# Turning the first two tiles on TensorE and computing the modulation as columns, in an adaLN block with a mixture-of-experts feed-forward

## The chip, the cores and the metric

The kernel runs on one core of one Trainium2 chip. The metric is the device time of one execution in microseconds (us). The engines are TensorE (PE; its weight loads are shown apart as PEld), VectorE (DVE), ScalarE (ACT), GpSimd (POOL) and SyncE (SP), which here only issues DMAs. Each engine works through its own instruction list in order; the lists meet in semaphores alone.

## The reference, cut to what matters

There are 4 batches of 1024 tokens with 512 channels, all in f32. A vector per batch gives six modulation vectors, two normalised inputs are shifted and scaled by them, and two branches are gated by them.

```
mod = silu(c) @ wmod                       # (4,512) @ (512,3072): sa, ca, ga, sb, cb, gb
ga, gb = clamped to |g| >= 0.25
h = layernorm(x) * (1 + ca) + sa
q, k, v = relu(h Wq), relu(h Wk), h Wv     # 16 heads of 32
vk = [v, 1]^T k over the tokens of a batch;  out = (vk q) / (its last row)
x = x + ga * (out Wproj + b)
h = layernorm(x) * (1 + cb) + sb
x = x + gb * (top-2-of-8 experts(h) + shared expert(h))
```

## The kernel before

Tokens are cut into 32 tiles of 128 (TILES; BT = 8 tiles make a batch). Numbers that enter a projection are split into a high and a low f16 part, so one product is three f16 matmuls (split_matmul, L85 to L89). The low part is what DVE (or POOL) subtracts after ACT wrote the high part.

All five engines run a written-out loop over slots s. In slot s PE projects tile s (project_k, project_v, project_q), then adds its keys and values into vk (sum_keys_values). From slot 9 on it also attends for tile t = s - 9 and projects out for tile t - 1. From slot 32 on the shared expert runs beside the last attention tiles, then alone, and the last stage runs 71 tiles of 128 expert slots: e_up, e_turn (three f32 transposes on PE), e_down.

The way of tile i to PE: DVE takes its statistics (stats) and writes (x - mean) * (1 + ca) (centre), ACT multiplies by the deviation (scale), POOL adds sa (shift), ACT writes the high part (h_high), DVE the low part (h_low), SP issues a transposing DMA into ht (turn_h). rows_f holds ca and sa of a batch, spread over all partitions. In slot s the engines do this for tile s + 2. DVE's list in a slot is q_low(s-1), centre(s+2), stats(s+3), k_low(s), h_low(s+2), v_low(s), and sum_keys_values(s) on PE waits for k_low(s) and v_low(s):

```
            pe.wait_ge(m.k_lo, i + 1)
            pe.wait_ge(m.v_lo, i + 1)
```

The start: four DMAs bring the first 1024 columns of wmod. PE multiplies them by silu(c) of batch 0 repeated over 128 columns (L1279), which gives sa and ca already spread over the partitions, in f32 matmuls that each show as two passes. It then computes modulation rows 0 and 1 for all four batches (modulate, L1238: weights 128x4, 512 columns stream through). Rows 2 and 3 follow in slot 3 and rows 4 and 5 in slot 4, each row in 4 matmuls, after sum_keys_values; ACT and DVE copy and clamp them as tiles of 4x512. In slot 6 SP stores them to DRAM and loads them back spread over the partitions (load_rows_b), then loads the first out-projection weights, and only then issues the transposing DMA of tile 8:

```
        if s == 6:
            sp.wait_ge(m.mod_step, 12)
            ...
            load_rows_b(0)
            load_xr(0)
            for k in (0, 1):
                load_wp(0, k)
        turn_h(s + 2)
```

The twelve pieces of the query, key and value weights (128x512 each) arrive in a ring and are split by ACT (split_high, L977) and DVE (split_low, L591) between the other work of the first slots. vk_low(b) on DVE (L525) writes the low part of a batch's vk at the end of slot 8(b+1), and attend in the next slot waits for it.

## Time and profile before

| what | us |
|---|---|
| median of 3 runs | 1217.57 |
| lowest and highest run | 1216.61 and 1219.41 |
| the profiled execution, its own time | 1217.89 |
| its span in the trace | 1216.1 |
| PE busy in the span | 1189.8 |
| DVE, ACT, POOL busy | 805.9, 417.7, 506.3 |

The span is what the trace covers; the execution's own time is 1.79 us longer. Busy time adds up stages with different limits, so it says which engine is the fullest and nothing about a single stage. Matmuls are pipelined, so a matmul's recorded duration is longer than the distance to the next one; the distance is what counts in a sum.

### The profile page before, as it was taken

The numbers are of one execution on the slowest core, as the hardware profiler recorded it, in microseconds if no ns is written. First come the engines' busy times: TensorE is split into PE (matmuls) and PEld (weight loads), VectorE is DVE, ScalarE is ACT, GpSimd is POOL, SyncE is SP. The second block draws the span as 40 slices with busy tenths as digits, with TensorE's granted clock in tenths as the row PEclk, the third lists the DMA queues.
The fourth block names the chain that finished last, engine by engine and source line by source line (L and its number), as shares of the span: only waits on it lengthen the run. The fifth ranks groups of instructions, "written<-read, shape, count | busy, mean of one in ns | idle before, by whom it ended". The sixth has DMA issues, their size and how long they took to land.

```text
span 1216.1 us, 25326 instructions
## 1 busy us (share of the span) xinstructions
PE 1189.8 (98%) x9054; PEld 776.8 (64%) x9054; DVE 805.9 (66%) x1578; ACT 417.7 (34%) x873; POOL 506.3 (42%) x409
## 2 busy tenths in 40 slices
PE   7999999999999999999999999999999999999996
PEld 2646666666666666767777777656666666666663
DVE  5647778878776777655857754266666666666665
ACT  4424444445443432333323323222222222222221
POOL 2212566656564554222112112345445554455543
PEclk9999999999999999999999999999999999999998
DMA  7816597998788978745434535579787897779783
GB/s 238 228 40 168 125 250 192 214 234 212 182 222 185 229 209 197 173 99 120 122 87 104 137 85 117 111 150 135 132 141 140 131 132 139 138 135 136 133 127 45
DMA packets 253255, 185.27 MB, mean 152 GB/s; under 512 B 186496, under 2 KB 198784, under 8 KB 253132
## 3 DMA queue, kind: packets, MB, share of 16 engines
q1 hardware_dynamic: 217368, 114.40, 42.1%
q0 software_dynamic: 20512, 45.62, 22.4%
q10 hardware_dynamic: 15256, 23.62, 6.7%
q8 instruction: 79, 1.29, 0.4%
q14 instruction: 40, 0.33, 0.1%
HBM read 87.07 MB, written 52.75 MB: 115 GB/s over the span
## 4 chain that ended last, share of the span: by engine, by line
PE 90%; DVE 2%; issue 2%; DMA 2%; POOL 1%; ACT 1%; SPq 0%; ACTq 0%; POOLq 0%; DVEq 0%
PE ps_o L87 7%; PE ps_o L89 7%; PE ps_o L88 7%; PE ps_vs L87 6%; PE ps_vs L88 6%; PE ps_vs L89 6%; PE ps_kh L87 4%; PE ps_vh L87 4%; PE ps_vh L88 4%; PE ps_vh L89 4%; PE ps_kh L88 4%; PE ps_kh L89 4%; PE ps_qh L87 4%; PE ps_qh L89 4%; PE ps_qh L88 4%
## 5 line engine op out<-in xcount | busy, mean ns | idle before, releaser
L444 POOL DMA_INDIRECT out<-y,slot_row x71 | 139.3, 1963 | 190.3 <-DVE y L882 138.7
L89 PE MATMUL ps_o<-w_all,xt 128*128 x568 | 177.5, 313 | 0.0
L88 PE MATMUL ps_o<-w_all,xt 128*128 x568 | 177.5, 313 | 0.0
L87 PE MATMUL ps_o<-w_all,xt 128*128 x568 | 177.5, 312 | 0.0
L874 DVE SCALAR_TENSOR_TENSOR gate_row<-gate_rows,batch_weight,gate_row 128x512 f32<-128x512 f32 x213 | 158.9, 746 | 2.5
L368 POOL DMA_INDIRECT out<-s_sum,row_no x32 | 53.8, 1680 | 197.6 <-DVE s_sum L623 192.0
L1133 ACT ACTIVATE at<-ps_y 128x384 f16<-128x384 f32 x71 | 34.8, 491 | 250.7 <-PE ps_y L1353 247.1
L330 POOL TENSOR_TENSOR h<-cen,rows_f 128x512 f32<-128x512 f32 x32 | 40.6, 1270 | 130.6 <-ACT cen L901 115.4
L89 PE MATMUL ps_qh<-ht,wqkv 128*128 128x128 f16 x512 | 87.4, 219 | 0.0
L88 PE MATMUL ps_qh<-ht,wqkv 128*128 128x128 f16 x512 | 87.4, 219 | 0.0
L87 PE MATMUL ps_qh<-ht,wqkv 128*128 128x128 f16 x512 | 87.4, 219 | 0.0
L864 DVE SCALAR_TENSOR_TENSOR a<-ps_o,a 128x352 f32<-128x352 f32 x71 | 37.3, 525 | 73.9 <-PE ps_o L89 72.6
L431 POOL DMA_INDIRECT g<-h_d,slot_token x71 | 71.9, 1013 | 31.9 <-issue 21.0
L882 DVE TENSOR_TENSOR y<-ps_vs,gate_row 128x512 f32<-128x512 f32 x71 | 49.1, 692 | 52.6 <-PE ps_vs L89 51.7
L87 PE MATMUL ps_vs<-w_all,at 128*128 (+1 forms) x213 | 80.9, 380 | 2.9 <-DVE at L869 2.9
L598 DVE SCALAR_TENSOR_TENSOR s_act<-ps_vh,s_act 128x256 f32<-128x256 f32 x32 | 13.6, 424 | 102.7 <-ACT s_act L984 102.6
L89 PE MATMUL ps_vs<-w_all,at 128*128 (+1 forms) x213 | 80.6, 378 | 0.0
L88 PE MATMUL ps_vs<-w_all,at 128*128 (+1 forms) x213 | 80.6, 378 | 0.0
L89 PEld LDWEIGHTS ps_o<-w_all,xt 128*128 128x128 f16 x568 | 55.6, 98 | 29.1
L88 PEld LDWEIGHTS ps_o<-w_all,xt 128*128 128x128 f16 x568 | 55.5, 98 | 26.4
L87 PEld LDWEIGHTS ps_o<-w_all,xt 128*128 128x128 f16 x568 | 55.4, 98 | 25.5
L87 PE MATMUL ps_kh<-s_ht,sh 128*128 128x256 f16 x256 | 69.8, 272 | 0.1
(251 smaller groups left out, 3341.2 us busy)
## 6 DMA issues: line engine op xcount, KB each, us to landing
w_stage<-in_w_d ACTq DMA_DIRECT2D x64, 176.0 KB
xb<-in_x SPq DMA_DIRECT2D x32, 256.0 KB, 3.7
xr<-in_x SPq DMA_DIRECT2D x32, 256.0 KB, 4.0
out<-x SPq DMA_DIRECT2D x32, 256.0 KB, 3.6
h_d<-hl SPq DMA_DIRECT2D x32, 256.0 KB, 2.5
h2t_d<-h2t SPq DMA_DIRECT2D x32, 256.0 KB, 3.5
s_ht<-h2t_d SPq DMA_DIRECT2D x32, 256.0 KB, 3.6
sstage<-in_sh_flat SPq DMA_DIRECT2D x32, 136.0 KB, 3.6
```

What stands on the lines that cost most here:

```text
L87: nc.tensor.matmul(out, lh, rh, start=first, stop=False, skip_group_check=True)
L88: nc.tensor.matmul(out, lh, rl, start=False, stop=False, skip_group_check=True)
L89: return nc.tensor.matmul(out, ll, rh, start=False, stop=last, skip_group_check=True)
L330: pool.tensor_tensor(m.h[:, i % 2, :], m.cen[:, i % 2, :], m.rows_f[:, (i // BT) % 2, SA, :], ALU.add).then_inc(m.h_done, 1)
L368: pool.indirect_dma_start(m.out, bass.IndirectOffsetOnAxis(ap=m.row_no[:, t:t + 1], axis=0), m.s_sum[:, u, :], None, compute_op=ALU.add).t ...
L431: pool.indirect_dma_start(m.g[r][:, :], None, m.h2_d, bass.IndirectOffsetOnAxis(ap=m.slot_token[:, t:t + 1], axis=0)).then_inc(m.gathered[ ...
L444: pool.indirect_dma_start(m.out, bass.IndirectOffsetOnAxis(ap=m.slot_row[:, t:t + 1], axis=0), m.y[:, t % Y_RING, :], None, compute_op=ALU ...
L598: v.scalar_tensor_tensor(out=m.s_act[:, q % 2, :], in0=m.ps_h[j % 3][:, 1, :], scalar=1.0 / SCALE, in1=m.s_act[:, q % 2, :], op0=ALU.mult, ...
L864: v.scalar_tensor_tensor(out=m.a[:, t % 2, 0:INTER], in0=m.ps_h3[:, 0:INTER], scalar=1.0 / SCALE, in1=m.a[:, t % 2, 0:INTER], op0=ALU.mult ...
L874: v.scalar_tensor_tensor(out=row, in0=m.gate_rows[:, b, :], scalar=m.batch_weight[:, b, t:t + 1], in1=row, op0=ALU.mult, op1=ALU.add).then ...
L882: v.tensor_tensor(m.y[:, t % Y_RING, :], m.ps_ey[:, 0:C], m.gate_row[t % GW_RING][:, :], ALU.mult).then_inc(m.ey_ready, 1)
L1133: act.activation(m.at[:, t % 2, 0, :, :], m.ps_a[:, :, :], ACT.Copy).then_inc(m.e_at_hi, 1)
```

## The change

Tiles 0 and 1 no longer go through POOL's shift and the transposing DMA. DVE normalises them (normalise), PE turns the result with four f32 transposes (turn_n), and DVE applies scale and shift as per-partition numbers, since a channel is now a partition (modulate_turned). ACT and DVE (POOL for tile 1) write the two f16 parts straight into ht.

For that the modulation is computed turned. A chunk of wmod (128x128, f32) is now the weight, and the four columns of silu(c) stream through. There are 96 such matmuls: 32 at the start, which give sa and ca, and 64 that are issued one by one behind each split_matmul of the projections of tiles 3, 4 and 5 (modulate_beside). Clamps and products work on 128x16. The rows that later stages need are made by one PE transpose each, in slot 0 and, for the rest, in slot 6 after project_v (turn_modulation), copied by ACT and then stored by SP. rows_f of batch 0 is made by POOL (a diagonal matrix) and PE (spread_rows) and copied by DVE and ACT.

The order of the first slots is written out anew. PE runs turn_n(1) and spread_rows(SA) after project_v(0). SP loads all twelve weight pieces through a ring of 8. DVE handles splits 0 to 11, k_low(0) and stats(2) ahead of the slot loop, with modulate_turned(1) between splits 8 and 9.

Three waits move at other places: vk_low of the last batch stands earlier in slot 32; the buffer at is two buffers, of which only the second waits for the shared expert's end; and the last e_turn is issued inside the e_down before it. The diff, cut to its core:

```diff
-X_RING, QT_RING, HT_RING, XR_RING, X2_RING, H2T_RING, STAGE_RING, W_RING = 4, 10, 3, 2, 3, 3, 6, 4
+X_RING, QT_RING, HT_RING, XR_RING, X2_RING, H2T_RING, STAGE_RING, W_RING = 4, 10, 3, 2, 3, 3, 8, 4
...
-CONSTS = 5
-SPLITS_FIRST = {-2: (4,), -1: (6,), 0: (10, 11)}
-SPLITS_LAST = {-2: (5,), -1: (7, 8, 9)}
+IDENT_READY, MODT_READY, V_READY, HEADS_READY = 3, 5, 7, 12
+PE_TURNED = 2
+MOD_GROUP, MOD_GROUPS, MODT = 8, 3, 32
+MOD_FROM, MOD_STEPS = 3, 24
...
+    for n in range(KC, 2 * KC):
+        sp.dma_start(m.stage[:, n, :], m.pieces[n][0]).then_inc(m.stage_loaded[n], 16)
     load_x(2)
+    for n in range(2 * KC, 3 * KC):
+        sp.wait_ge(m.stage_lo, n - STAGE_RING + 1)
+        sp.dma_start(m.stage[:, n % STAGE_RING, :], m.pieces[n][0]).then_inc(m.stage_loaded[n % STAGE_RING], 16)
...
         if s == 6:
-            sp.wait_ge(m.mod_step, 12)
-            sp.dma_start(m.mod_d[:, 2 * C:6 * C], m.mod[:, 2 * C:6 * C]).then_inc(m.mod_stored, 16)
-            sp.dma_start(m.gab_d, m.gate_tmp[:, 0:C]).then_inc(m.mod_stored, 16)
-            sp.wait_ge(m.mod_stored, 48)
+            sp.wait_ge(m.modrow_copied, 2)
+            sp.dma_start(m.mod_f_d.rearrange("b (c n) -> (b c) n", n=P), m.modrow[:, 1, :]).then_inc(m.mod_stored, 16)
+            sp.wait_ge(m.mod_stored, 32)
...
+        if s == -2:
+            pool.wait_ge(m.mod_copied, 2)
+            for r, cols in ((CA, SCALE_A), (SA, SHIFT_A)):
+                pool.tensor_tensor(m.diag[:, r, :, :], m.ident[:, :].unsqueeze(1).to_broadcast([P, KC, P]),
+                                   m.modt[:, 0, cols].unsqueeze(2).to_broadcast([P, KC, P]), ALU.mult).then_inc(m.diag_done, 1)
+        if s == -1:
+            pool.wait_ge(m.h_hi, 2)
+            pool.tensor_tensor(m.ht[:, 1, KC:2 * KC, :], m.h[:, 1, :].rearrange("p (k n) -> p k n", k=KC), m.ht[:, 1, 0:KC, :],
+                               ALU.subtract).then_inc(m.h_lo, 1)
...
+    def normalise(i):
+        v.wait_ge(m.rstd_done, i + 1)
+        v.tensor_scalar(m.cen[:, i, :], m.xb[:, i, :], m.mv[:, i, 0:1], m.rstd[:, i, :], ALU.subtract, ALU.mult).then_inc(m.cen_done, 1)
+
+    def modulate_turned(i):
+        v.wait_ge(m.n_turned, i + 1)
+        for k in range(KC):
+            op = v.tensor_scalar(m.h[:, i, k * P:(k + 1) * P], m.ps_n[i][:, k, :], m.modt[:, 0, 4 + k:5 + k], m.modt[:, 0, k:k + 1], ALU.mult, ALU.add)
+            op.then_inc((m.scaled, m.h_half, m.h_half, m.h_done)[k], 1)
+
+    def turned_low(half):
+        part = slice(2 * half, 2 * half + 2)
+        v.wait_ge((m.h_half_hi, m.h_hi)[half], 1)
+        v.tensor_tensor(m.ht[:, 0, KC + 2 * half:KC + 2 * half + 2, :], m.h[:, 0, :].rearrange("p (k n) -> p k n", k=KC)[:, part, :],
+                        m.ht[:, 0, part, :], ALU.subtract).then_inc((m.h_half, m.h_lo)[half], 1)
...
+    stats(0)
+    normalise(0)
+    split_low(0)
+    split_low(1)
+    v.wait_ge(m.mod_done, 1)
+    v.wait_ge(m.consts, MODT_READY)
+    v.tensor_scalar(m.modt[:, :, SCALE_A], m.ps_mod[0][:, SCALE_A, :].rearrange("p c b -> p b c"), 1.0, None, ALU.add).then_inc(m.mod_copied, 1)
+    v.tensor_copy(m.modt[:, :, SHIFT_A], m.ps_mod[0][:, SHIFT_A, :].rearrange("p c b -> p b c")).then_inc(m.mod_copied, 1)
+    v.wait_ge(m.mod_copied, 2)
+    modulate_turned(0)
+    split_low(2)
+    turned_low(0)
+    split_low(3)
+    turned_low(1)
+    split_low(4)
+    split_low(5)
+    stats(1)
+    split_low(6)
+    split_low(7)
+    normalise(1)
+    split_low(8)
+    modulate_turned(1)
+    for n in range(9, 12):
+        split_low(n)
+    k_low(0)
+    stats(2)
+    for s in range(TILES + TAIL):
         t = s - LAG
-        if s == -3:
-            v.wait_ge(m.silu_done, 1)
-            for k in range(KC):
-                v.tensor_copy(m.sct_rep[:, k, :], m.sct[:, k, 0:1].to_broadcast([P, P])).then_inc(m.rep_done, 1)
-        if s == -2:
-            v.wait_ge(m.bc_done, 2)
-            v.tensor_scalar(m.rows_f[:, 0, CA, :], m.ps_o[:, 1, :], 1.0, None, ALU.add).then_inc(m.row0_done, 1)
+        if s == 0:
+            v.wait_ge(m.bc_done, 1)
+            v.tensor_copy(m.rows_f[:, 0, CA, :], m.ps_row[CA]).then_inc(m.row0_done, 1)
...
+        if s == TILES:
+            vk_low(B - 1)
         h2_low(t - 2)
-        for n in SPLITS_LAST.get(s, ()):
-            split_low(n)
         v_low(s)
...
-        if 0 < s <= TILES and s % BT == 0:
+        if 0 < s < TILES and s % BT == 0:
...
+    def turned_high(i, part, ready, done):
+        act.wait_ge(ready, i + 1)
+        act.activation(m.ht[:, i, part, :], m.h[:, i, :].rearrange("p (k n) -> p k n", k=KC)[:, part, :], ACT.Copy).then_inc(done, 1)
...
+    turned_high(0, slice(0, 2), m.h_half, m.h_half_hi)
+    turned_high(0, slice(2, 4), m.h_done, m.h_hi)
+    for n in range(KC, 2 * KC + 1):
+        split_high(n)
...
+    k_high(0)
+    turned_high(1, slice(0, 4), m.h_done, m.h_hi)
+    for n in range(2 * KC + 1, 3 * KC):
+        split_high(n)
...
+        if s in m.mod_slots:
+            g = m.mod_slots[s]
+            chunks = slice(MOD_GROUP * g, MOD_GROUP * (g + 1))
+            act.wait_ge(m.mod_done, g + 1)
+            act.activation(m.modt[:, :, chunks], m.ps_mod[g][:, :, :].rearrange("p c b -> p b c"), ACT.Copy).then_inc(m.mod_copied, 1)
+        if s in m.turn_slots:
+            r = m.turn_slots[s]
+            act.wait_ge(m.modrow_done, r + 1)
+            act.activation(m.modrow[:, r, :], m.ps_modrow[r], ACT.Copy).then_inc(m.modrow_copied, 1)
...
-        if t == 0:
+        if t == 1:
...
+            if i < PE_TURNED:
+                pe.wait_ge(m.h_lo, i + 1)
+            else:
+                pe.wait_ge(m.ht_loaded[i % HT_RING], ht_use(i))
             at_least(pe, m.k_lo, i)
-            if i == 0:
-                pe.wait_ge(m.stage_lo, KC)
             for k in range(KC):
+                if i == 0:
+                    pe.wait_ge(m.stage_lo, k + 1)
                 mm = split_matmul(nc, m.ps_k[:, :], (m.ht[:, i % HT_RING, k, :], m.ht[:, i % HT_RING, KC + k, :]),
                                   (m.wqkv[:, k, 0, C:2 * C], m.wqkv[:, k, 1, C:2 * C]), k == 0, k == KC - 1)
-            mm.then_inc(m.k_done, 1)
+                if k == KC - 1:
+                    mm.then_inc(m.k_done, 1)
+                modulate_beside(i, k)
...
+    def modulate(n):
+        g, k, c = n // (MOD_GROUP * KC), n // MOD_GROUP % KC, n // (MOD_GROUP * KC) * MOD_GROUP + n % MOD_GROUP
+        if g == 0 and n % MOD_GROUP == 0:
+            pe.wait_ge(m.wmod_loaded[k], 16)
+        if g > 0 and n % (MOD_GROUP * KC) == 0:
+            pe.wait_ge(m.wmod_loaded[KC + g - 1], 16 * KC)
+            pe.wait_ge(m.h_done, PE_TURNED)
+            pe.wait_ge(m.modrow_copied, 1)
+        mm = nc.tensor.matmul(m.ps_mod[g][:, n % MOD_GROUP, :], m.wmod[:, k, c * P:(c + 1) * P], m.sct[:, k, :],
+                              start=k == 0 and c == MOD_GROUP * g, stop=k == KC - 1, skip_group_check=True)
+        if (n + 1) % (MOD_GROUP * KC) == 0:
+            mm.then_inc(m.mod_done, 1)
+
+    def modulate_beside(i, step):
+        n = MOD_GROUP * KC + MOD_STEPS * (i - MOD_FROM) + step
+        if MOD_FROM <= i and n < MOD_GROUPS * MOD_GROUP * KC:
+            modulate(n)
+
+    def turn_n(i):
+        pe.wait_ge(m.consts, IDENT_READY)
+        pe.wait_ge(m.cen_done, i + 1)
         for k in range(KC):
-            pe.wait_ge(m.wmod_loaded[KC * (j // 2) + k], 16)
-            mm = nc.tensor.matmul(m.ps_mod[j], m.sct[:, k, :], m.wmod[:, k, j * C:(j + 1) * C], start=k == 0, stop=k == KC - 1)
-        mm.then_inc(m.mod_done, 1)
+            mm = nc.tensor.transpose(m.ps_n[i][:, k, :], m.cen[:, i, k * P:(k + 1) * P], m.ident[:, :])
+        mm.then_inc(m.n_turned, 1)
+
+    def spread_rows(r):
+        pe.wait_ge(m.diag_done, 1 if r == CA else 2)
+        nc.tensor.matmul(m.ps_row[r], m.one[:, :], m.diag[:, r, :, :].rearrange("p k n -> p (k n)"), start=True, stop=True).then_inc(m.bc_done, 1)
+
+    def turn_modulation(r):
+        mm = nc.tensor.transpose(m.ps_modrow[r], m.modt[:, :, :].rearrange("p b c -> p (b c)"), m.ident[:, :])
+        mm.then_inc(m.modrow_done, 1)
...
-    pe.wait_ge(m.rep_done, KC)
-    for k in range(KC):
-        pe.wait_ge(m.wmod_loaded[k], 16)
-        for r in (0, 1):
-            mm = nc.tensor.matmul(m.ps_o[:, r, :], m.sct_rep[:, k, :], m.wmod[:, k, r * C:(r + 1) * C], start=k == 0, stop=k == KC - 1)
-            if k == KC - 1:
-                mm.then_inc(m.bc_done, 1)
-    modulate(0)
-    pe.wait_ge(m.row0_done, 2)
-    modulate(1)
+    pe.wait_ge(m.silu_done, 1)
+    for n in range(MOD_GROUP * KC):
+        modulate(n)
+    turn_n(0)
+    spread_rows(CA)
 
     for s in range(TILES + TAIL):
         t = s - LAG
         project_k(s)
         project_v(s)
+        if s == 0:
+            turn_n(1)
+            spread_rows(SA)
+        if s == 6:
+            pe.wait_ge(m.mod_step, 12)
+            turn_modulation(1)
...
-        for j in m.mod_slots.get(s, ()):
-            if j == 2:
-                pe.wait_ge(m.row0_done, 2)
-            if j == 3:
-                pe.wait_ge(m.mod_copied, 2)
-            if j >= 4:
-                pe.wait_ge(m.mod_copied, j - 1)
-            modulate(j)
+        if s == 0:
+            pe.wait_ge(m.h_done, PE_TURNED)
+            turn_modulation(0)
...
+    def e_down(t, expert, turn_within=False):
         pe.wait_ge(m.e_at_lo, t + 1)
         at_least(pe, m.ey_ready, t)
         for k in range(IT):
+            if turn_within and k == 1:
+                e_turn(t + 1)
...
-    pe.wait_ge(m.consts, CONSTS)
     expert = expert_of(0)
     e_up(0, expert)
     down(CHUNKS - 1)
...
         e_up(t, following)
         if t == 1:
             pe.wait_ge(m.s_t1_done, 2 * CHUNKS)
-        e_down(t - 1, expert)
+        e_down(t - 1, expert, t == SLOT_TILES - 1)
         expert = following
-    e_turn(SLOT_TILES - 1)
...
+    m.at = [(sb, region(GATE_AT, ACT_AT))[j](f"at{j}", [P, 2, IT, P], F16) for j in range(2)]
...
+        m.mod_slots, m.turn_slots = {4: 1, 5: 2}, {0: 0, 6: 1}
```

## Rows read from the trace of the kernel before

**Rows 1.** Chain that ended last, first 26 us: start us, length us, what.

```profile
5.89 10.12 PE ps_o L1279 x16
...
16.77 0.76 DVE cen L486
...
18.36 1.27 POOL h L330
19.66 0.64 ACT hl L908
...
21.04 4.33 DMA ht<-hl
25.41 0.46 PE ps_kh L87
```

**Rows 2.** Busy: PE, PEld, DVE, ACT, POOL; then granted clock, DMA share, GB/s.

```profile
25.40:28.90 3.50, 3.48 (x9) 1.29 (x10) 3.50 (x6) 1.72 (x4) 0.38 (x2) 0.53 0.99 238
```

**Rows 3.** The same chain, slots of tiles 0 to 6.

```profile
32.46 0.06 PE ps_qh L87
...
35.14 0.06 PE ps_vs L1197
...
35.82 0.22 PE ps_kh L87
...
44.37 0.22 PE ps_kh L87
...
77.08 6.96 PE ps_o L1238 x16
...
92.69 0.22 PE ps_kh L87
```

**Rows 4.** PE weight loads in time: start us, length us, line, tiles, form.

```profile
11.15 0.33 PEld L1279 LDWEIGHTS ps_o<-wmod,sct_rep 128*128 128x128 f32 x1 [0.52 <-issue]
11.98 0.19 PEld L1279 LDWEIGHTS ps_o<-wmod,sct_rep 128*128 128x128 f32 x1 [0.50 <-issue]
```

**Rows 5.** PE weight loads by shape: count, busy us, mean ns, idle before.

```profile
L89 PEld LDWEIGHTS ps_qh<-ht,wqkv 128*128 128x128 f16 x512 | 50.1, 98 | 0.0
...
L1238 PEld LDWEIGHTS ps_o<-wmod,sct 128*4 128x4 f32 x32 | 2.6, 87 | 9.8 <-issue 9.6
```

**Rows 6.** PE matmuls in order of time, router logits of one tile.

```profile
307.26 0.17 PE L1231 MATMUL ps_o<-gate,h2t 128*128 128x16 f16 x1
...
307.44 0.17 PE L1232 MATMUL ps_o<-gate,h2t 128*128 128x8 f16 x1
```

**Rows 7.** DVE groups by line and shape.

```profile
L497 DVE SCALAR_TENSOR_TENSOR k_sb<-ps_kh,k_sb 128x512 f16<-128x512 f32 x32 | 22.1, 690 | 12.2 <-ACT k_sb L914 12.1
...
L537 DVE TENSOR_SCALAR den<-ps_o 128x16 f32<-128x16 f32 x32 | 5.3, 164 | 0.0
```

**Rows 8.** DVE in order of time, a split while POOL works.

```profile
23.58 1.34 DVE L591 SCALAR_TENSOR_TENSOR wqkv<-stage,wqkv 128x512 f16<-128x512 f32 x1 [0.30 <-ACT wqkv L977]
```

**Rows 9.** SP's DMA issues in slot 6: start us, length us, line, tiles.

```profile
94.47 0.29 SPq L265 DMA_DIRECT2D gab_d<-gate_tmp  x1
96.96 0.34 SPq L202 DMA_DIRECT2D rows_ga<-mod_d  x1
...
100.24 1.24 SPq L161 DMA_TRANSPOSE ht<-hl  x1
```

**Rows 10.** Tile ht, the transposing DMA issued at 100.24 us alone.

```profile
DMA to landing us min/median/max: 6.5/6.5/6.5
```

**Rows 11.** Tile ht, all its DMAs of the first 140 us.

```profile
DMA to landing us min/median/max: 3.0/4.1/8.7
```

**Rows 12.** PE waits, 354 to 450 us: waiter, releaser, total, times, longest.

```profile
PE ps_o L87 <- DVE vk L525: 2.5, 1, 2.5
```

**Rows 13.** Waits of the whole span, one of ScalarE.

```profile
ACT gate_row L1139 <- DMA gate_rows<-mod_d: 12.2, 1, 12.2
```

**Rows 14.** The same chain, last 20 us, its last turn.

```profile
1203.28 0.34 PE ps_y L1353 x3
```

More of the change, by code:

```diff
@@ L64 @@
 VK_OPS = 6
-MODS = 6
 class Parts:
@@ L89, in split_matmul, with ht_use @@
     return nc.tensor.matmul(out, ll, rh, start=False, stop=last, skip_group_check=True)
+def ht_use(i):
+    return 16 * len(range(i % HT_RING if i % HT_RING >= PE_TURNED else i % HT_RING + HT_RING, i + 1, HT_RING))
 def rows_of(dram, i):
@@ L157, in turn_h @@
     def turn_h(i):
-        if tile(i):
+        if tile(i) and i >= PE_TURNED:
             sp.wait_ge(m.h_lo, i + 1)
@@ L326, in shift @@
     def shift(i):
-        if tile(i):
+        if tile(i) and i >= PE_TURNED:
             pool.wait_ge(m.scaled, i + 1)
@@ L371, in gpsimd_program @@
     step(pool.memset(m.minus_half[:, :], -0.5))
+    step(pool.memset(m.ident[:, :], 0.0))
+    step(pool.affine_select(out=m.ident[:, :], in_=m.ident[:, :], compare_op=ALU.not_equal, fill=1.0,
+                            base=0, pattern=[[-1, P]], channel_multiplier=1))
+    step(pool.memset(m.one[:, :], 1.0))
+    step(pool.memset(m.modt[:, :, :], 0.0))
     step(pool.memset(m.v_sb[:, :, 0, :, P:P + 1], SCALE))
@@ L480, in centre @@
     def centre(i):
-        if tile(i):
+        if tile(i) and i >= PE_TURNED:
             if i % BT == 0 and i:
@@ L663, in vector_program @@
         stats(s + 3)
-        if s == -3:
-            for n in range(KC):
-                split_low(n)
-        for n in SPLITS_FIRST.get(s, ()):
-            split_low(n)
         if s == 1:
@@ L897, in scale @@
     def scale(i):
-        if tile(i):
+        if tile(i) and i >= PE_TURNED:
             act.wait_ge(m.cen_done, i + 1)
```

165 lines of the change are left out of this document (68 added, 97 removed).

## The prediction

> **What bounds the kernel now.** I read the page first: TensorE is busy for nearly the whole span, so a part of the change counts for what it does to TensorE's list, and other engines count where TensorE waits for them. The chain of waits then shows three places that the change touches. At the start it runs through the first f32 matmuls on TensorE, VectorE, ScalarE, GpSimd, ScalarE, VectorE and a transposing DMA, and the first projection begins at 25.41 us [rows 1]. From there it stays on TensorE, 8.55 us a tile (35.82 to 44.37), broken only by the wide modulation matmuls of slots 3 and 4, 6.96 us each [rows 3]. The waits name one stall further on, 2.5 us for vk_low of the last batch [rows 12]. The end hangs on the last e_turn and what follows it [rows 14].
>
> The sum is made against the profiled execution, 1217.89 us, whose span is 1216.1 us. The median of the three runs is 1217.57 us, so what the sum changes is put on that. Within 0.2% (2.4 us) this kernel's measurement can hardly tell a change from none.
>
> **A thin f32 pass.** The new modulation loads 128x128 f32 weights and streams four columns. No row shows that shape. A weight load of 128 f32 columns took 0.19 us, one of 4 columns 0.087 us [rows 4, 5], so the part that grows with columns is 0.103 us, 0.107 us for 128. The early load of 0.33 us [rows 4] is longer by about twice that part; while TensorE runs at the lower of its levels I take 0.213 us. The rest of a load overlaps its neighbours: f16 loads last 0.098 us [rows 5], yet eight f16 passes of 16 and 8 columns with such loads start within 0.18 us, 0.026 us apart [rows 6]. That 0.026 is the lower bound for the distance of two thin passes, the full 0.19 (0.33) the upper; I take 0.107 (0.213), since the durations follow the columns.
>
> **The first group.** Removed: 16 passes of 512 columns that gave sa and ca, and 16 for modulation rows 0 and 1. Added: 32 matmuls, 64 thin passes, which can start at the same 5.89 us [rows 1]. The load row changes from 0.33 to 0.19 us by 11.98 us [rows 4]; if the level rises there again, 29 passes are done by then and 35 follow at 0.107: the group ends at 15.8 us. Bounds: 64 at 0.026 and its double give 7.6 to 9.2 us, 0.33 then 0.19 gives 20.6 us.
>
> **From there to the first projection.** Four transposes and their latency, 0.75 us (three take 0.34 [rows 14]). Four VectorE operations on 128x128, between 0.164 and 0.69 us each [rows 7]; I take 0.28, started 0.2 apart: 0.9. Then split_low(2), half of the low part, split_low(3), the other half: about 1.95 us by the 0.69 of 128x512. GpSimd makes the two diagonals meanwhile, and a split took 1.34 us beside GpSimd's work [rows 8]; I add 0.6 (0 to 1.3). Project_k(0) starts 4.2 us after the group, at 20.0 instead of 25.41. GpSimd's diagonal (1.27 [rows 1]) and spread_rows(CA) fit into these 4.2 us.
>
> **What is late next.** Project_k(0) and project_v(0) took 25.41 to 32.46, 7.05 us [rows 1, 3], so they now end at 27.0, 5.4 us earlier. Only then does turn_n(1) stand in TensorE's list, and VectorE, in order, is stopped at modulate_turned(1) until it is done. Behind that instruction are queued splits 9 to 11, k_low(0), stats(2), the copy of rows_f, centre(2), stats(3), h_low(2) and, last, v_low(0), for which sum_keys_values(0) waits. Counted from the end of project_v(0): transposes 0.64; four operations, 1.5; ScalarE's high part of tile 1 and split 9 at 0.64 each [rows 1], 2.8; three splits on VectorE, 4.65; k_low, 5.25; stats, 6.25; copy, 6.95; centre(2) to the end of h_low(2) took 16.77 to 21.04, 4.27 us [rows 1], 11.2; v_low, 11.8; with GpSimd beside it 12.2. TensorE has project_q(0) in between (waiting for splits 10 to 12) and then nothing for some 5 us. Before, this distance was 32.46 to 35.14, 2.7 us [rows 3]. So sum_keys_values(0) starts at 39.2 instead of 35.14: 4.05 us later. After the wait ahead of the first projection TensorE's granted clock was 0.53 for 3.5 us [rows 2]; the new wait is longer, so I count that loss once more, 3.5 x 0.47 = 1.65. The start costs 5.7 us. Its bounds follow from the group's end, and from 0 to 1.65 for the clock.
>
> The weight loads by SP cost nothing: project_v and project_q still wait for VectorE's splits. Tile 2's transposing DMA is issued 11.2 us after project_v(0) and needed some 22 us after it, so even 8.7 us to landing [rows 11] is covered.
>
> **Modulation beside the projections.** Removed: two groups of 16 wide passes, 13.92 us [rows 3]. Added: 64 matmuls. 24 stand behind matmuls of 512 columns, which hide the first load; exposed are 0.107 and two floors of 0.026, 0.16 us each. 40 stand behind matmuls of 128 columns, 0.055 apart, which hide half the first load: 0.107 + 0.052 + 0.052, 0.21 us each. 3.8 + 8.4 = 12.2 us, a gain of 1.7 us. At 0.026 a pass it is 3.3 us (gain 10.6), at 0.19, with 0.05 for the floors, it is 24 x 0.24 and 40 x 0.38 less what 0.055 hides, 20.8 (loss 6.9). The shorter clamps are work of VectorE while TensorE is the bound: nothing.
>
> By the Trainium skill, "TensorE: Matmul & The Clock Gate", section "LDWEIGHTS (loading the stationary operand)", a load takes its columns divided by 1.2 in ns, an estimate of 107 ns for 128 columns, with no word of the engine's level. The rows agree at the higher level and show about twice as much at the lower one [rows 4]. By the rule the sum below would come to +0.5 instead of +3.5 us, because the first group would end at 12.7 us. The section "Weight-path perf modes — Fast Weight Load (FWL) and DoubleRow" says that the fast load is not used for f32 weights; that speaks against the first rival.
>
> **Slot 6.** SP's store waited only for VectorE's clamps and went out 1.8 us after project_k(6) began (94.47 against 92.69 [rows 3, 9]). Now turn_modulation(1) comes after project_v(6), 5.2 us, and ScalarE copies it behind v_high and sh_high: 6.6 us. From store to tile 8's transposing DMA SP took 94.47 to 100.24, 5.8 us [rows 9], so that is issued at 12.4 and, with the 6.5 us to landing of this very DMA [rows 10], lands at 18.9. Project_k(8) is due after two tiles, 17.1. Loss 1.8 us; 0 at the median landing of 4.1, 3.7 at 8.7 [rows 11] and a bit of latency. Rows_b and the out-projection weights come later too, but are not needed for two more slots.
>
> **The moved waits.** Vk_low early in slot 32 ends the stall of 2.5 us [rows 12]: VectorE has the value from ScalarE by then, and nothing else is late at that attend. Gain 2.5, at worst 0. The two at buffers: nothing, because ScalarE is held there by the load of the gate rows anyway, its one wait of 12.2 us [rows 13]. The last e_turn, 0.34 us [rows 14], is earlier on TensorE, but VectorE reads its result only after e_out of the tile before, which now waits for 0.34 us more of TensorE: loss 0.2 (0 to 0.4).
>
> **Sum.** 5.7 - 1.7 + 1.8 - 2.5 + 0.2 = +3.5 us: 1221.4 for the profiled execution, 1221.1 for the median.
>
> **Rivals.**
> First, faster: the thin passes flow as the f16 ones do. At 0.026 the group ends 6.6 us earlier and slots 3 to 5 save 8.9 more, 1205.6 us. For it: loads are taken ahead and f16 loads hide all but 0.026. Against it: 0.087 for 4 columns and 0.19 for 128. It decides from about 0.076 us a pass downwards (-2.4 us), where 1215.2 is reached.
> Second, no change: the passes are 0.107 apart from the beginning, whatever the level. Then the group ends at 12.7, 3.0 us earlier: 1218.1. The change then only moves the waiting from ahead of the first projection to behind it. Against it: the 0.33 us rows.
> Third, slower still: the level stays low through the first group, since no row shows a stretch of thin passes at either level. 64 x 0.213 ends at 19.5, and the transposes take 0.4 more: +4.1, 1225.2.
> Fourth: a thin pass costs its whole recorded load. The group ends at 20.6 (+4.8) and slots 3 to 5 lose 8.6 more: 1234.5.
>
> **How the numbers follow.** The forecast has 0.34 (alone 1218.5 to 1223.5), the first rival 0.20, the second 0.18, the third 0.22, the fourth 0.06. Faster: the first rival and a little of the second, 0.24. Within 0.2% (1215.1 to 1220.0): the rest of the second and the lower edge of the forecast, 0.25. Slower: 0.51. The range runs from 1208 to 1226: it takes in both neighbours and most of the first rival, and leaves out the fourth and a pass under 0.04 us.
>
> **What would show it.** Right: weight loads of the new modulate line 0.2 us apart at first and 0.11 later; project_k(0) near 20 us; turn_n(1) after project_v(0); TensorE idle until v_low near 39 us; tiles 3, 4 and 5 together 12 us longer than their neighbours; a short wait of TensorE for ht at tile 8; no wait for vk near 403 us. Wrong: a sum_keys_values(0) before 36 us, tiles 3 to 5 less than 8 us longer, or a wait of another kind in slots 6 to 9.

## The result and the profile after

The changed kernel took 1237.10 us in the median of 4 runs (1236.25 to 1238.97), the kernel before 1217.55 us (1216.61 to 1219.41): 1.0161 times as long (95% interval 1.0143 to 1.0179), 19.6 us more. The prediction was 1221.1 us with a range of 1208 to 1226. The direction was right; the time lies 11 us above the range, and a single measurement of either kernel varies by 1 to 2 us around its median.

The profiled execution after took 1238.97 us, the slowest of the four, with a span of 1236.9 us, 20.8 us more than before. This table follows the loss through the span. A time is the start of the named step among TensorE's instructions in order of time; the last column is what the stretch ending there added.

| step | before | after | later by | stretch |
|---|---|---|---|---|
| project_k(0) | 25.41 | 24.05 | -1.4 | -1.4 |
| project_k(1) | 35.66 | 44.95 | 9.3 | +10.7 |
| project_k(3) | 52.75 | 63.73 | 11.0 | +1.7 |
| project_k(6) | 92.53 | 100.35 | 7.8 | -3.2 |
| project_k(8) | 109.62 | 119.31 | 9.7 | +1.9 |
| project_k(10) | 127.41 | 141.23 | 13.8 | +4.1 |
| first matmul of the shared expert | 391.67 | 405.97 | 14.3 | +0.5 |
| its second step in slot 33 | 419.50 | 435.38 | 15.9 | +1.6 |
| first matmul on an expert's input | 780.68 | 796.07 | 15.4 | -0.5 |
| start of the 6th e_down, settled again | 826.56 | 846.98 | 20.4 | +5.0 |
| last matmul | 1206.61 | 1227.29 | 20.7 | +0.3 |

The start, which the prediction put at 5.7 us, shows in the chain of the kernel after (start us, length us, what); it answers to [rows 1].

```profile
5.91 13.78 PE ps_y L1295 x64
19.69 0.97 PE ps_o L1309 x4
...
24.05 0.61 PE ps_kh L88
...
31.49 0.45 PE ps_o L1309 x4
...
31.96 1.38 DVE h L515 x4
...
34.54 2.44 DVE wqkv L626 x3
...
41.37 2.78 issue
```

The 64 thin passes (L1295) are 0.215 us apart to the end, so the group ends at 19.69. The transposes of tile 1 come only at 31.49, and VectorE stands still for 3.50 us until they are done:

```profile
31.96 1.36 DVE L515 TENSOR_SCALAR h<-ps_o,modt 128x128 f32<-128x128 f32 x4 [3.50 <-PE ps_o L1309]
...
43.37 0.69 DVE L538 TENSOR_TENSOR v_sb<-ps_vh,v_sb 128x512 f16<-128x512 f32 x1
```

The splits behind that push project_q(0) back by 2.9 us, and TensorE then stands for 2.78 us more until v_low(0), the second of these lines, is done.

TensorE's waits of the kernel after (waiter, releaser, total, times, longest) name the rest.

```profile
PE ps_vs L88 <- DVE at L914: 5.6, 2, 4.3
PE ps_vs L1249 <- issue: 5.1, 2, 2.8
PE ps_qh L88 <- DVE wqkv L626: 2.9, 1, 2.9
PE ps_y L88 <- DMA ot<-ol: 2.2, 2, 2.0
PE ps_kh L88 <- DMA ht<-hl: 1.6, 1, 1.6
```

The kernel before has this line for the wait for at:

```profile
PE ps_vs L87 <- DVE at L869: 2.9, 2, 1.6
```

Compared with it, vk is gone from the list [rows 12], tile 8's ht, ot and two stalls ahead of sum_keys_values (2.8 us for tile 0, 2.3 for tile 8) are new, and the wait for at at the first e_down has grown from 1.60 to 4.3 us. Behind five of the waits TensorE ran at its lower level. The next rows give stretches of TensorE (busy, granted clock, DMA share, GB/s): project_q(0), sum_keys_values(0) and what follows, slots 3 to 5, sum_keys_values(8) and on, the out-projection in slot 34, the first e_down.

```profile
35.83:41.37 5.54, 5.34 (x45) 0.50 0.00 0
44.15:48.58 4.43, 4.43 (x23) 0.64 1.08 290
63.73:100.35 36.62, 36.62 (x383) 1.00 0.30 82
129.62:133.96 4.34, 4.34 (x22) 0.62 0.85 204
430.89:434.35 3.46, 3.46 (x9) 0.53 0.92 289
815.32:819.00 3.68, 3.68 (x9) 0.50 0.99 193
```

How slot 6 costs more than tile 8's wait is in SP's issues (answering to [rows 9]) and in ScalarE in order of time, both of the kernel after:

```profile
106.84 0.33 SPq L274 DMA_DIRECT2D mod_f_d<-modrow  x1
...
112.31 2.59 SPq L166 DMA_TRANSPOSE ht<-hl  x1
114.95 0.58 SPq L155 DMA_DIRECT2D xb<-in_x  x1
115.57 0.47 SPq L160 DMA_DIRECT2D sstage<-in_sh_flat  x1
```

```profile
114.39 0.60 ACT L969 ACTIVATE v_sb<-ps_vh 128x512 f16<-128x512 f32 x1 [1.13 <-PE ps_vh L90]
121.60 0.43 ACT L980 ACTIVATE sh<-sstage 128x272 f16<-128x272 f32 x1 [6.61 <-DMA sstage<-in_sh_flat]
121.94 0.61 ACT L1013 ACTIVATE wproj<-wp_raw 128x512 f16<-128x512 f32 x1
122.46 0.58 ACT L975 ACTIVATE qt<-ps_qh 128x512 f16<-128x512 f32 x1
```

SP's store goes out 6.5 us after project_k(6) begins (1.9 us before). ScalarE then stands for 6.61 us in slot 7, and its copies of q, k and v come late for sum_keys_values(8).

### The profile page after: what moved, and what is told of

Same layout as the page of the kernel before. It is cut to its first block, busy times and chain, and to the rows that moved or that the text cites. A ratio compares the mean times of both kernels' runs of the same rounds, so it can differ in the third digit from the quotient of the medians.

```text
span 1236.9 us, 25609 instructions
## 1 busy us (share of the span) xinstructions
PE 1199.4 (97%) x9196; PEld 802.3 (65%) x9196; DVE 798.5 (65%) x1583; ACT 413.6 (33%) x871; POOL 506.6 (41%) x412
## 4 chain that ended last, share of the span: by engine, by line
PE 87%; DVE 3%; issue 3%; DMA 3%; SPq 1%; POOL 1%; ACT 1%; ACTq 0%; POOLq 0%; DVEq 0%
PE ps_o L88 7%; PE ps_o L90 7%; PE ps_o L89 7%; PE ps_vs L88 6%; PE ps_vs L89 6%; PE ps_vs L90 6%; PE ps_kh L88 4%; PE ps_kh L90 4%; PE ps_kh L89 4%; PE ps_vh L88 4%; PE ps_vh L89 4%; PE ps_vh L90 4%; PE ps_qh L88 4%; PE ps_qh L89 4%; PE ps_qh L90 4%
## 5 line engine op out<-in xcount | busy, mean ns | idle before, releaser
L88 PE MATMUL ps_qh<-ht,wqkv 128*128 128x128 f16 x512 | 91.3, 221 | 3.1 <-DVE wqkv L626 2.9
L90 PE MATMUL ps_qh<-ht,wqkv 128*128 128x128 f16 x512 | 91.5, 222 | 0.0
L89 PE MATMUL ps_qh<-ht,wqkv 128*128 128x128 f16 x512 | 91.5, 222 | 0.0
L339 POOL TENSOR_TENSOR h<-cen,rows_f 128x512 f32<-128x512 f32 x30 | 38.0, 1268 | 111.2 <-ACT cen L946 99.0
```

The costliest lines, as they stand in the source:

```text
L88: nc.tensor.matmul(out, lh, rh, start=first, stop=False, skip_group_check=True)
L89: nc.tensor.matmul(out, lh, rl, start=False, stop=False, skip_group_check=True)
L90: return nc.tensor.matmul(out, ll, rh, start=False, stop=last, skip_group_check=True)
L339: pool.tensor_tensor(m.h[:, i % 2, :], m.cen[:, i % 2, :], m.rows_f[:, (i // BT) % 2, SA, :], ALU.add).then_inc(m.h_done, 1)
```

## The experiments

My theory after the traces: four separate waits (the start, slot 6, ot in slot 34, the rows at the expert switch), less 3 us gained beside the projections. Rivals for each stand in the expectations. Ratios are to the kernel before, measured beside each run, with 95% intervals; its medians were 1217.1 to 1218.8 us. An interval is 1.3 to 2.3 us to either side, so two changed kernels that differ by 3 us are barely apart, and which wait went is read from the traces.

**vk_alone**, the moved vk_low in the kernel before:

```diff
+        if s == TILES:
+            vk_low(B - 1)
         h2_low(t - 2)
...
-        if 0 < s <= TILES and s % BT == 0:
+        if 0 < s < TILES and s % BT == 0:
             vk_low(s // BT - 1)
```

> The kernel before with one part of the change: vk_low of the last batch stands before h2_low in slot 32. My prediction's term: TensorE's stall of 2.5 us for vk goes, nothing else is late, so the time falls by 2.5 us (about 1215.0). Rival, from the trace of the changed kernel: the stall only moves. VectorE's later instructions in slots 32 and 33 are no earlier, so the transposing DMA of the next out-projection (ot) is as late as before, and TensorE waits there instead: about 0.6 us left at attend, some 2 us at the out-projection, and the 3.5 us that follow run at the lower level, which costs 1.6 us: between -0.5 and +1.6 us against before.

0.9990 (0.9978 to 1.0001): some 1 us or nothing. TensorE's waits in this run:

```profile
PE ps_y L87 <- DMA ot<-ol: 1.1, 1, 1.1
...
PE ps_o L87 <- issue: 0.7, 2, 0.4
```

The stall of 2.5 us shrank to 0.4 and 1.1 us came back at ot: the rival's mechanism, at a smaller price, since the level did not fall behind it here. The way to ot hangs on GpSimd's list, as the chain of the kernel after shows:

```profile
421.78 1.26 POOL h L350
423.04 1.23 POOL xg L358
...
424.31 1.26 POOL ol L363
...
425.59 5.26 DMA ot<-ol
```

In that execution the level fell behind the wait for ot, and the stretch from the first matmul of the shared expert took 1.6 us longer than before. It is the exception. The six other traces of kernels with the moved vk_low and the rows of the changed kernel have a wait of 1.8 to 2.0 us there too, with the level at 1.00 behind it, and the stretch takes 27.5 to 27.8 us against 27.8 before; one of them, slot6_later:

```profile
427.40:430.90 3.50, 3.48 (x27) 1.00 0.98 307
```

So in the changed kernel the move gained next to nothing, and the 1.6 us are the profiled execution's own.

**at_alone**, the buffers, their wait and the last e_turn in the kernel before:

```diff
-        if t == 0:
+        if t == 1:
             act.wait_ge(m.s_t1_done, 2 * CHUNKS)
...
-    m.at = region(GATE_AT, ACT_AT)("at", [P, 2, 2, IT, P], F16)
+    m.at = [(sb, region(GATE_AT, ACT_AT))[j](f"at{j}", [P, 2, IT, P], F16) for j in range(2)]
```

> The kernel before with the two at buffers, the wait for the shared expert's end at the second of them, and the last e_turn inside the e_down before it; nothing else of the change. My prediction's term: 0 for the buffers and +0.2 us for the e_turn, 1217.8. Rival: the buffers are what lengthens the wait of TensorE at the first e_down from 1.60 to 4.27 us in the changed kernel, with 2.4 us at the lower level behind it: +5.0 us, 1222.6, with a wait of some 4 us for at in the trace. A third view: that wait follows the landing of the gate rows (12.2 us of waiting by ScalarE before, 14.9 after), which these buffers do not touch; then this run shows about 1.6 us there as before.

0.9998 (0.9988 to 1.0009), wait at the first e_down 1.66 us: the buffers leave this wait as it was, and the time within 1.5 us. The counterpart is **after_old_at**, the changed kernel with this part of the diff (without the e_turn) taken back:

> The changed kernel with the single at buffer and its old wait (the e_turn inside e_down stays). If the two buffers make the 4.27 us wait at the first e_down, it goes back to about 1.6 us and the time falls by 5 us, to about 1232. If it is the landing of the gate rows, the wait stays at some 3 to 4 us where the gate rows take 9 us to land, or is shorter in this execution only because they land earlier: 1237 within 1 us.

1238.06 us, 1.0162 (1.0144 to 1.0180), wait 4.68 us. The buffers are not what lengthens the wait; ScalarE's wait for the gate rows was 15.3 us here.

**before_rows16.** In the kernel before, the batches' modulation rows lie 6 x 512 numbers, 12 KB, apart in DRAM; in the changed kernel 32 x 128, 16 KB.

```diff
-    m.mod_d, m.gab_d = dram("mod_d", (B, 6 * C), F32), dram("gab_d", (B, C), F32)
+    m.mod_d, m.gab_d = dram("mod_d", (B, 8 * C), F32), dram("gab_d", (B, C), F32)
```

> The kernel before, only the DRAM tensor that holds the modulation rows is laid out 16 KB from batch to batch (as in the changed kernel) instead of 12 KB. If that layout is what makes the gate rows land late at the switch to the experts (ScalarE's wait for them was 14.9 to 15.3 us in three traces with the 16 KB rows and 12.0 to 12.3 us in three with 12 KB), the wait of TensorE at the first e_down grows from 1.6 to about 4.3 us, with 2.4 us at the lower level behind it: 1222.6. If it is something else of the change, 1217.6, within 1 us, with the wait at 1.6 us.

1222.27 us, 1.0037 (1.0023 to 1.0051): 4.5 us slower by one number. The number also makes the tensor larger, which rows_padded tells apart. Its waits, of TensorE and of ScalarE:

```profile
PE ps_vs L87 <- DVE at L869: 6.1, 2, 4.8
...
ACT gate_row L1139 <- DMA gate_rows<-mod_d: 15.4, 1, 15.4
```

ScalarE's wait before was 12.2 us [rows 13]. **rows_padded** goes the other way, the changed kernel with 18 KB:

```diff
-    ... dram("mod_f_d", (B, MODT * P), F32)
+    ... dram("mod_f_d", (B, MODT * P + C), F32)
...
-            sp.dma_start(m.mod_f_d.rearrange("b (c n) -> (b c) n", n=P), m.modrow[:, 1, :]).then_inc(m.mod_stored, 16)
+            for b in range(B):
+                sp.dma_start(m.mod_f_d[b, 0:MODT * P].rearrange("(c n) -> c n", n=P), m.modrow[b * MODT:(b + 1) * MODT, 1, :]).then_inc(m.mod_stored, 16)
```

> The changed kernel, only the DRAM tensor of the modulation rows has 18 KB from batch to batch instead of 16 KB (the store is four DMAs then). In the kernel before, 16 instead of 12 KB cost 5 us: the gate rows landed late. If it is the distance of 16 KB, ScalarE's wait for the gate rows goes back to about 12.2 us and the wait at the first e_down to about 1.6 us, with no lower level behind it: 5 us less, 1232; the out-projection's wait for ot in slot 34, during which s_gb is read from the same rows, may shrink by 1 us more. If it is that the rows lie in a larger tensor or come from another place, the wait stays near 4.3 us and the time at 1237.

1233.64 us, 1.0133 (1.0118 to 1.0149): 3.5 us less than the changed kernel. The waits for at and for the gate rows are back at 1.8 and 12.4 us with a still larger tensor, and the wait for ot has shrunk from 2.0 to 1.0 us, as the expectation had it. Against that the four stores hold tile 8's DMA longer:

```profile
PE ps_kh L88 <- DMA ht<-hl: 4.2, 1, 4.2
...
PE ps_vs L88 <- DVE at L915: 3.1, 2, 1.8
...
ACT gate_row L1183 <- DMA gate_rows<-mod_f_d: 12.4, 1, 12.4
```

**slot6_later** and **slot6_weights_too.** The first moves SP's block one slot on; the second moves the weights' split as well.

```diff
-        if s == 6:
+        if s == 7:
             sp.wait_ge(m.modrow_copied, 2)
...
-    return ((0, 0),) if s == 7 else ((0, 1),) if s == 8 else ((0, 2), (0, 3)) if s == 9 else ()
+    return ((0, 0), (0, 1)) if s == 8 else ((0, 2), (0, 3)) if s == 9 else ()
...
-        if 8 <= s <= 9:
-            load_wp(0, s - 6)
+        if s == 9:
+            load_wp(0, 2)
+            load_wp(0, 3)
```

> The changed kernel, but SP's block with the store of the modulation rows, the loads of rows_b, xr and the out-projection weights stands in slot 7, behind the transposing DMA of tile 8 and the load of the next shared-expert piece, and ahead of the transposing DMA of tile 9. Theory from the trace after: the block held back two things, tile 8's DMA (TensorE waits 1.6 us) and the shared piece for which ScalarE stands still for 6.6 us, with its copies of k, v and q behind it (TensorE waits 2.3 us more and then runs 4.3 us at the lower level): 5.9 us in all, so about 1231.2. My prediction's view, that only tile 8's DMA is late: 1.8 us, 1235.3. Rival: the transfers are slow because many are in flight (6.95 us for tile 8's), then the place in the list changes nothing by more than 1 us, 1237.

1234.68 us, 1.0133 (1.0114 to 1.0152). Tile 8's wait is gone; the stall ahead of sum_keys_values(8) stays at 2.45 us, though nothing runs at the lower level behind it. From project_k(6) to project_k(10) this is 3.3 us less than after. The shared piece is in time now, and the next instruction on ScalarE's list is what waits, in order of time:

```profile
115.14 0.42 ACT L980 ACTIVATE sh<-sstage 128x272 f16<-128x272 f32 x1
120.58 0.63 ACT L1013 ACTIVATE wproj<-wp_raw 128x512 f16<-128x512 f32 x1 [5.02 <-POOL wp_raw L370]
121.11 0.58 ACT L975 ACTIVATE qt<-ps_qh 128x512 f16<-128x512 f32 x1
```

> The changed kernel with SP's block in slot 7 as in the run that moved it, and the first out-projection weights split one slot later as well (two pieces in slot 8, two in slot 9, loads accordingly). The trace of that run showed ScalarE standing still 5.0 us in slot 7 for the product of the first weight piece, which waits for the rows, with its copies of q, k and v behind it, and TensorE's stall of 2.4 us ahead of sum_keys_values(8) unchanged. If that is the second half of what slot 6 costs, the stall goes: 2.5 us less than that run, with nothing left of the lower level there: about 1231.5. If the second pair of weights is now late for the first out-projection, a wait of 1 to 3 us appears in slot 10 and the time is 1233 to 1235.

1231.80 us, 1.0125 (1.0108 to 1.0142). No wait of TensorE from 95 to 150 us is left, and nothing is late in slot 10. Slot 6 had cost 5.3 us by the medians, 5.9 us in the traces from project_k(6) to project_k(10): the block held back tile 8's DMA, the shared piece and the first weights, one behind the other.

**turn1_early** and **start_reordered.** The first turns tile 1 ahead of project_k(0), and for that takes its statistics and normalises it ahead of the modulation; the second also moves v_high(0), v_low(0) and the copy of ca's row ahead of tile 2's way.

```diff
     split_low(1)
+    stats(1)
+    normalise(1)
...
     turn_n(0)
     spread_rows(CA)
+    turn_n(1)
...
         if s == 0:
-            turn_n(1)
             spread_rows(SA)
```

```diff
     k_low(0)
+    v_low(0)
     stats(2)
```

> The changed kernel, with tile 1 normalised ahead of the modulation and turned right after spread_rows(CA), ahead of project_k(0), instead of behind project_v(0). My prediction's step says that VectorE is held at modulate_turned(1) by project_v(0) and that everything behind it (splits 9 to 11, k_low, h_low(2), v_low) is late by that: in the trace after VectorE stood still for 3.5 us there. Then sum_keys_values(0) starts 3.4 us earlier (40.7 instead of 44.2) and the time falls by about 3.4 us, to 1233.7. Rival: the start is lost to the lower level of the first group alone, and VectorE catches up in any case: then 1237 within 1 us.

1232.32 us, 1.0125 (1.0108 to 1.0142): sum_keys_values(0) at 39.2 us and project_k(3) 5.1 us earlier than after. The step on turn_n(1) holds. VectorE, in order of time:

```profile
27.00 1.37 DVE L517 TENSOR_SCALAR h<-ps_o,modt 128x128 f32<-128x128 f32 x4
...
38.41 0.69 DVE L540 TENSOR_TENSOR v_sb<-ps_vh,v_sb 128x512 f16<-128x512 f32 x1
```

Modulate_turned(1) and v_low(0) both come 4.96 us earlier than after, with the same distance between them. 3.5 us are the stall that is gone; the other 1.5 are stats(1) and normalise(1), which now fill the time in which VectorE waits for the modulation. Project_q(0) runs at 1.00 here instead of 0.50, which gains nothing, since TensorE then waits longer for v_low(0).

> The changed kernel with tile 1 turned early as in the other run, and v_high(0), v_low(0) and the copy of the row of ca ahead of stats(2), centre(2) and h_low(2). If v_low(0) behind the way of tile 2 is the other half of the stall, sum_keys_values(0) starts right behind project_q(0), at about 35 us, project_k(1) at 35.7 as before; tile 2's transposing DMA is then the next that is late, issued near 40.5 and landing near 45: project_k(2) at 45 to 46 instead of 55.2, about 9 us less than the changed kernel, 1228. Rival: the DMA takes 8 us or TensorE stays at the lower level after that wait: project_k(2) at 49 to 50, 1232.

1233.67 us, 1.0143 (1.0127 to 1.0160). Sum_keys_values(0) starts at 34.07 and project_k(1) at 34.9, as expected, and then the stall moves to tile 2, in order of time:

```profile
42.73 0.23 PE L88 MATMUL ps_qh<-ht,wqkv 128*128 128x128 f16 x1 [2.51 <-DVE qt L546]
47.62 0.22 PE L1255 MATMUL ps_vs<-v_sb,k_sb 128*128 128x129 f16 x1 [2.04 <-DVE v_sb L540]
51.02 0.61 PE L88 MATMUL ps_kh<-wqkv,ht 128*128 128x512 f16 x1 [2.27 <-DMA ht<-hl]
```

The rival's time, and 0.0018 more than turn1_early, within the intervals; project_k(3) comes 2.9 us later than there. I read it so that the start lacks VectorE's time for tile 2, wherever the order puts it; no run shows that by itself.

**warmed_first**, 18 wide matmuls ahead of the group:

```diff
+    for n in range(18):
+        nc.tensor.matmul(m.ps_k[:, :], m.warm[:, 0:P], m.warm[:, :], start=True, stop=True, skip_group_check=True)
     pe.wait_ge(m.silu_done, 1)
     for n in range(MOD_GROUP * KC):
```

> The changed kernel with 18 more f16 matmuls of 512 columns on a constant ahead of the first group, into a bank that is not yet in use; TensorE has nothing else to do until 5.9 us, and the 18 take about 7.7 us at the lower level, so the group starts some 2.7 us later. If TensorE gets to its higher level by being busy with wide matmuls and the thin passes keep it there, the passes are 0.107 us apart instead of 0.215 and the group ends near 15.5 us instead of 19.7: about 4 us less, 1233, and project_k(0) runs at the higher level too. If thin passes fall back to the lower level, or their distance has nothing to do with it, the group ends at 22.4 us: 1239 to 1240.

1233.68 us, 1.0135 (1.0119 to 1.0150), 3.4 us less. Windows of TensorE in this run (the count is of matmuls started; the first window is of wide ones):

```profile
4.40:5.40 1.00, 1.00 (x5) 1.00 1.02 377
7.40:8.40 1.00, 1.00 (x11) 1.00 1.02 418
10.40:11.40 1.00, 1.00 (x11) 1.00 1.06 399
11.40:12.40 1.00, 1.00 (x8) 0.64 1.05 389
12.40:13.40 1.00, 1.00 (x6) 0.50 1.04 385
```

Both views hold in part: the thin passes, which begin at 6.98 us, run at 11 a microsecond, 0.09 us apart, once the wide ones have brought the higher level; between 11.4 and 12.4 us the level falls, with TensorE never idle. The group ended at 16.3 us, 3.35 us earlier than after. That the time fell by as much is in part luck. Project_k(0) still began at the lower level (0.50 from 20.70 to 24.00), and at project_k(3) only 1.2 us of the gain were left:

```profile
62.53 0.39 PE L88 MATMUL ps_kh<-wqkv,ht 128*128 128x512 f16 x1 [1.15 <-DMA ht<-hl]
```

Another 2.4 us came between project_k(6) and project_k(10), where the stall ahead of sum_keys_values(8) was 1.05 instead of 2.3 us with no lower level behind it.

**three_mended** joins turn1_early, slot6_weights_too and rows_padded; **mended_and_warmed** adds the 18 matmuls.

> The changed kernel with three of its waits mended: tile 1 turned early, SP's block and the first out-projection weights one slot later, the rows at 18 KB. If the costs are separate and add up, as the single runs have them (4.8, 5.3 and about 5 us), 1237.1 falls to 1222, still slower than before by the rest of the start (some 6 us at project_k(3)) less what the modulation beside the projections gave back. If they overlap, 1226 or more.

1222.55 us, 1.0043 (1.0029 to 1.0057), with nothing of 1 us or more left in slots 1 to 31. By the ratios that is 14.4 us less than the changed kernel, where the three alone took 4.4, 4.4 and 3.4 us off: within the intervals the costs add up.

> The same three mends and the 18 wide matmuls ahead of the first group. If the first group at the lower level is the rest of what the start lost, and VectorE's list behind it moves up as a whole, another 4 us: 1218, level with the kernel before. If VectorE's list is the limit of the start whatever TensorE does, the earlier end of the group is worth less than 2 us: 1220 to 1222.

1220.73 us, 1.0028 (1.0015 to 1.0041); runs from 1217.8 to 1224.7. That is the second outcome's time, but it is not clear of three_mended, and in the trace project_k(3) came 2.3 us earlier than there, between the two. In the profiled execution, at 1224.71 the slowest of eleven, the gate rows were late although they lie 18 KB apart:

```profile
PE ps_vs L88 <- DVE at L919: 8.1, 2, 6.8
...
ACT gate_row L1187 <- DMA gate_rows<-mod_f_d: 17.4, 1, 17.4
```

**mended_warmed_rows14**, the same with MODT = 28 instead of the 18 KB, and **gates_together**, the kernel before with the gate rows in one block of 8 KB and one load:

```diff
-    for b in range(B):
-        sp.dma_start(m.gate_rows[:, b, :], m.mod_d[b, 5 * C:6 * C].partition_broadcast(P)).then_inc(m.gates_loaded, 16)
+    sp.dma_start(m.gate_rows.rearrange("p b c -> p (b c)"), m.gb_d.rearrange("b c -> (b c)").partition_broadcast(P)).then_inc(m.gates_loaded, 16)
```

> The kernel mended_and_warmed with the rows 14 KB from batch to batch (28 chunks instead of 32, one store instead of four) in place of 18 KB. If the distance decides, with 16 KB the bad one, the wait at the first e_down is 1.6 us and the runs gather at 1217 to 1218. If the landing of these rows varies whatever the distance, the runs spread by some 6 us again, between 1217 and 1224.

1220.19 us, 1.0010 (0.9994 to 1.0027), runs from 1216.65 to 1224.63, wait 2.22 us in the profiled one. Beside it the kernel before spread from 1215.9 to 1223.4 too, so the spread decides nothing.

> The kernel before, with the four gate rows also stored as one block of 8 KB and loaded with one DMA instead of four that lie 12 KB apart. If what counts is that all partitions read the same few short rows from places far apart, the one DMA lands earlier than 7.5 us after its issue, ScalarE's wait of 12.2 us gets shorter and TensorE's wait of 1.6 us at the first e_down goes: up to 1.6 us less, 1216. If the megabyte of data sets the landing, nothing changes: 1217.3 within 0.5 us. If the longer reads from one place are slower, the wait grows as with the 16 KB rows: 1219 to 1222.

0.9993 (0.9981 to 1.0006), wait 1.16 us: one load is no faster than four by more than can be measured.

**beside_alone** keeps the start of the kernel before and computes only the other four vectors as columns; **best_of_both** adds the moved vk_low.

```diff
+                modulate_beside(i, k)
...
-        if s == 6:
-            sp.wait_ge(m.mod_step, 12)
+        if s == 7:
+            sp.wait_ge(m.mod_copied, 5)
```

> The kernel before with its own start and its own rows for sa and ca; only the other four modulation vectors are computed as columns beside the projections of tiles 3 to 5, with SP's block in slot 7 and the first out-projection weights one slot later, and rows 12 KB apart. My prediction's term for the 64 matmuls was -1.7 us (12.2 against 13.9); the tile distances of the changed kernel say 11.0, so -2.9, and one transpose of 0.1 us: 1214.5. Rival: TensorE falls to its lower level among the thin passes or something of slot 6 is still late: no gain, 1217 or more.

0.9992 (0.9977 to 1.0007): neither the gain that was expected nor a loss is shown by the time. From project_k(3) to project_k(8) it took 53.82 us, before 56.87: the 3.05 us are there in the trace. From the first matmul of the shared expert to its second step in slot 33 it took 2.1 us longer than before (TensorE's wait for vk was 3.2 us, and the granted clock 0.72 for 4 us behind it).

> The same with vk_low of the last batch moved as in vk_alone (which gave 1.1 us in its trace). If the two are independent, 4 us less than before: 1213.3. If the earlier attend only meets a later ot, 1214.5.

1215.49 us, 0.9981 (0.9967 to 0.9994): 2.3 us faster than before, the only version that beats both kernels beyond its interval. Its wait for ot is 2.6 us: the first of the two outcomes for vk_low did not come. The stretch from the first matmul of the shared expert takes 29.3 us, against 29.9 in beside_alone and 27.8 before.

## Why the prediction was wrong, by its own steps

- **The first group.** The step that failed is "if the level rises there again, 29 passes are done by then and 35 follow at 0.107: the group ends at 15.8 us". It ended at 19.69, the third rival's 19.5, which had a chance of 0.22. The sum let the level rise where it had risen in the kernel before, under wide passes; here 64 thin passes did not raise it, and warmed_first shows that they do not even hold it. What a pass took at each level was sized well, 0.215 measured against 0.213 and 0.09 against 0.107, with some luck: by the rows the early load is longer than the one of 4 columns by 0.243 us, 2.4 times 0.103 and not twice. By the Trainium skill, "TensorE: Matmul & The Clock Gate", section "LDWEIGHTS (loading the stationary operand)", the columns divided by 1.2 give the load in ns, an estimate of 107 ns for 128 columns; the trace is near it at the higher level (0.09 us in warmed_first) and at twice that in the first group (0.215 us).
- **From there to sum_keys_values(0).** Right within half a microsecond each: project_k(0) 4.4 us behind the group (4.2), 7.4 us for project_k(0) and project_v(0) (7.05), sum_keys_values(0) 12.7 us behind project_v(0) (12.2), 1.8 us more from there to project_k(3) than before (1.65 for the lower level). With the group's end these make 11.0 us where the sum had 5.7. The step that VectorE is held at modulate_turned(1) is shown by turn1_early.
- **Modulation beside the projections.** The term was mis-sized by 1.5 us: 11.0 us for the 64 matmuls (4.2, 4.2 and 2.6 a tile) instead of 12.2, and the 14.1 us that the distances before show instead of 13.92: -3.2, not -1.7. At 0.17 us a matmul the first rival (0.05) and the fourth (0.33) are out. Beside projections the level holds, 1.00 from 63.73 to 100.35.
- **Slot 6.** Tile 8's wait was sized right (+1.9 against 1.8). What failed is "Rows_b and the out-projection weights come later too, but are not needed for two more slots". TensorE does not need them, but ScalarE's list has the split of the first weight, and ahead of it that of a shared piece, in slot 7, in front of the copies of q, k and v. That made 4.1 us more. It is the prediction's own sign of being wrong, "a wait of another kind in slots 6 to 9".
- **vk_low.** The step that failed is "nothing else is late at that attend": true of the attend, it missed the next wait, ot, whose way runs through GpSimd's list and comes no earlier. -1.9 at the attend and +1.95 at ot, next to nothing in place of a gain of 2.5; the +1.6 at the lower level belong to the profiled execution alone.
- **The at buffers.** Nothing, as predicted (at_alone), with the reason given there: ScalarE waits for the gate rows. The prediction took that wait of 12.2 us as given, and it is the one that grew. **The last e_turn:** +0.3 (0.2).
- **Not in the sum at all:** the layout of the rows in DRAM, 5.0 us at the expert switch, and 2.4 of these at the lower level. The diff shows the new shape; I priced the stores and not the reads. One constant, 16 KB from batch to batch for 12, is shown to do it in the kernel before. All eight traces with 16 KB have a wait of 4.0 to 4.8 us, all five with 12 KB one of 0.5 to 1.9 us. Why, and why the rows were late once at 18 KB, stays open.

With the third rival's first group alone the forecast would have been 1225.2 us, inside the range; slot 6, vk_low and the rows took the time out of it. In the profiled execution the span grew by 20.8 us where the sum had 3.5; the 17.3 us missed are the start with 5.3 (3.9 of it the group's end), slot 6 with 4.2, vk_low with 4.1 (1.6 measured, in this execution, against a gain of 2.5) and the rows with 5.0, less 1.5 for the modulation; the other stretches of the table make up less than 0.2 together.

## What to carry to other kernels

When a DMA or a wait moves past a point in one queue, go through every instruction behind it on every engine that it feeds, in list order, also those whose result is not needed soon: an in-order engine makes the next tile's copies wait for them. A stall taken away on the bounding engine is only worth what the next wait on the same path leaves, and a wait can cost more behind it: the lower level took 2.4 us after the wait of 4.3 us for at and 1.6 us after one of two for ot, and nothing after others of the same length. A change of shape in a DRAM buffer is a part of the change like any other: price its reads.
